# Sparse attention in a decoder kernel: alternating PSUM pairs for the first scores, a later key spreading, and the second thresholds in one piece

## The reference

```python
def sparsemax(x):
    x = x - jnp.max(x, axis=-1, keepdims=True)
    zs = -jnp.sort(-x, axis=-1)
    L = x.shape[-1]
    rho = jnp.arange(1, L + 1, dtype=x.dtype)
    cssv = jnp.cumsum(zs, axis=-1) - 1.0
    support = zs > cssv / rho
    k = jnp.maximum(jnp.sum(support, axis=-1, keepdims=True), 1)
    tau = jnp.take_along_axis(cssv, k - 1, axis=-1) / k.astype(x.dtype)
    return jnp.clip(x - tau, 0.0)
...
scores = jnp.einsum('bhqd,bhkd->bhqk', qh, kh) * scale
attn = sparsemax(scores)
out = jnp.einsum('bhqk,bhkd->bhqd', attn, vh)
...
return out @ Wo + bo
```

## Time and profile before

| what | value |
|---|---|
| median of 3 runs | 1659.28 us (1658.39 to 1662.68) |
| the profiled execution | 1649.06 us |
| its span, first to last instruction | 1647.3 us |
| mean granted TensorE clock over it | 0.795 of full speed |
| stage L3x within the span | about 1332.7 to 1475.5 us |

### The profile page before, as it was taken

The page is one execution under the profiler, slowest core; times in us unless marked ns, Lnnn a source line. Parts: engine busy times, 40 slices in busy tenths (PEclk is TensorE's granted clock), DMA queues, the critical chain, the costliest instruction groups (busy, mean ns, idle before and its releaser), DMA issues. The chain is left out here.

```text
span 1647.3 us, 35633 instructions
## 1 busy us (share of the span) xinstructions
PE 1186.9 (72%) x14064; PEld 904.8 (55%) x14064; DVE 1056.5 (64%) x2853; ACT 625.0 (38%) x1479; POOL 616.3 (37%) x694
## 2 busy tenths in 40 slices
PE   6982518957999779664687843299948875677778
PEld 5652417846788646553455733188825642564556
DVE  4988611148999748824688498243389937766672
ACT  2641103415777646122454321022124434443433
POOL 3437354432333236443233026533343343233320
PEclk9995559979999889676788555599958766777878
DMA  8900035660000085031000000355310000000000
GB/s 272 151 2 2 15 105 164 190 177 4 3 3 3 2 132 80 10 97 46 1 1 2 27 1 17 110 163 169 124 52 1 2 1 1 1 2 1 1 1 27
DMA packets 72010, 89.13 MB, mean 54 GB/s; under 512 B 5823, under 2 KB 59138, under 8 KB 71200
## 3 DMA queue, kind: packets, MB, share of 16 engines
q1 hardware_dynamic: 65824, 76.89, 18.6%
q0 software_dynamic: 6016, 9.93, 1.7%
HBM read 56.55 MB, written 32.69 MB: 54 GB/s over the span
## 5 line engine op out<-in xcount | busy, mean ns | idle before, releaser
L769 POOL TENSOR_TENSOR arena<-arena,small 128x1024 f32<-128x1024 f32 x80 | 154.7, 1939 | 112.1 <-ACT arena L651 65.8
L380 POOL TENSOR_SCALAR var_eps<-moments 128x1 f32<-128x1 f32 (+1 forms) x136 | 35.7, 262 | 356.5 <-DVE moments L373 356.5
L700 ACT ACTIVATE arena<-arena 128x1024 f32<-128x1024 f32 x80 | 84.7, 1058 | 135.0 <-DVE arena L844 134.9
L566 PE MATMUL ps<-arena,q 64*64 64x512 f32 x640 | 102.6, 714 | 40.4 <-issue 17.2
L576 PEld LDWEIGHTS ps<-small,arena 128*128 128x128 f32 x640 | 82.6, 159 | 63.9 <-issue 34.0
L725 ACT COPY arena<-ps 128x512 f32<-128x512 f32 x160 | 87.1, 588 | 68.2 <-PE ps L576 67.6
L576 PE MATMUL ps<-small,arena 128*128 128x128 f32 x640 | 100.5, 308 | 9.7 <-ACT arena L700 9.7
L1608 PEld LDWEIGHTS ps<-expert_ring,arena 128*128 128x128 f32 (+1 forms) x864 | 104.6, 192 | 2.9
L1608 PE MATMUL ps<-expert_ring,arena 128*128 128x128 f32 (+1 forms) x864 | 104.8, 275 | 0.0
L588 PEld LDWEIGHTS ps<-vx,arena 128*64 128x64 f32 x2560 | 90.8, 151 | 16.5 <-issue 13.2
L588 PE MATMUL ps<-vx,arena 128*64 128x18 f32 x2560 | 99.0, 222 | 0.9 <-issue 0.6
(11 more groups left out here) (363 smaller groups left out, 2946.6 us busy)
## 6 DMA issues: line engine op xcount, KB each, us to landing
expert_ring<-L2f_in SPq DMA_DIRECT2D x23, 704.0 KB, 4.2
expert_ring<-L0f_in SPq DMA_DIRECT2D x23, 578.0 KB, 3.9
slots_L0f<-blank SPq DMA_DIRECT2D x1, 8385.0 KB, 51.2
slots_L2f<-blank SPq DMA_DIRECT2D x1, 8385.0 KB, 49.9
small<-small_in SPq DMA_DIRECT2D x1, 4231.5 KB, 19.2
expert_ring<-L1f_in SPq DMA_DIRECT2D x8, 512.0 KB, 3.8
arena<-slots_L0f SPq DMA_DIRECT2D x23, 129.0 KB, 3.3
arena<-slots_L2f SPq DMA_DIRECT2D x23, 129.0 KB, 3.5
```

The source lines that it names most:

```text
L566: last = pe.matmul(c.ps[part(b), m], c.q[part(m), at:at + S], kx(t)[part(m), b * 512:(b + 1) * 512], start=True, stop=True)
L700: act.activation(buf(k), buf(k), ACT.Exp, scale=exp_scale).then_inc(s.probs_ready, 1)
L769: g.tensor_tensor(kx(t).rearrange("p (b h k) -> p b h k", b=2, k=S), bcast(of_tile, 2, HEADS // 2), bcast(bcast(c.w("head_of_row"), 2, S), ...
```

## The change

Four places of `sparse_attention` are edited.

- The scores of tiles 0 to 7 alternate between PSUM banks 0, 1 and banks 2, 3; later tiles use banks 0 and 1 as before. Up to tile 8, `scores(t)` waits for the copy of tile t-2 instead of tile t-1.
- On POOL, the spreading of tile 9 (and so of all later tiles) waits until the scan of the first half has ended (`s.summed`). Tile 8 is still spread ahead of that wait.
- `find_thresholds(1)` moves from the end of DVE's step 8 to the end of step 7, right behind `sum_largest(1)`. PE's `count_open_rows(1)` moves from the end of step 9 to the end of step 8.
- In DVE's step 9, `normalise(7)` moves behind `settle_thresholds(1)` and `less_threshold(8)`.

No instruction that computes is added or removed.

```diff
-    scores_ps = c.ps[:, 0:2].rearrange("p m n -> p (m n)")
+    score_banks = lambda t: 2 * (t % 2) if t < half_tiles else 0
+    scores_ps = lambda t: c.ps[:, score_banks(t):score_banks(t) + 2].rearrange("p m n -> p (m n)")
...
-            if t > 0:
-                pe.wait_ge(s.scored, t)
+            copied = t - 1 if t <= half_tiles else t
+            if copied > 0:
+                pe.wait_ge(s.scored, copied)
             for m in range(2):
                 for b in range(2):
                     at = t % 8 * P + b * S
-                    last = pe.matmul(c.ps[part(b), m], c.q[part(m), at:at + S],
+                    last = pe.matmul(c.ps[part(b), score_banks(t) + m], c.q[part(m), at:at + S],
                                      kx(t)[part(m), b * 512:(b + 1) * 512], start=True, stop=True)
...
-            if k == half_tiles + 1:
+            if k == half_tiles:
                 count_open_rows(1)
...
-            act.copy(z(t), scores_ps).then_inc(s.scored, 1)
+            act.copy(z(t), scores_ps(t)).then_inc(s.scored, 1)
...
         for t in range(1, half_tiles + 2):
+            if t == half_tiles + 1:
+
+                g.wait_ge(s.summed, 1)
             spread_keys(t)
...
                 if k == half_tiles + 1:
-                    normalise(tile_at(k - lag - 1))
                     settle_thresholds(1)
                     less_threshold(tile_at(k))
+                    normalise(tile_at(k - lag - 1))
                 less_threshold(tile_at(k + 1))
...
             if k == half_tiles - 1:
                 sum_largest(1)
-            if k == half_tiles:
                 find_thresholds(1)
```

## The result

The changed kernel took 1646.06 us in the median (1633.62 to 1649.62) against 1660.98 for the kernel before. The ratio is 0.989, with a 95% interval of 0.985 to 0.993. Two later comparisons, on a chip each and with more executions, gave 0.991 (0.9874 to 0.9945) and 0.991 (0.9877 to 0.9948), so some 15 us. Executions that took over 1.5% more than the fastest of the same kernel are left out of all ratios and medians.

What follows compares the result with a forecast made beforehand. No engine bounds the stage everywhere: scores wait for ACT's copy, POOL's spreading blocks DVE, later thresholds alternate between PE and DVE. Gains 5.2 + 3.3 + 2.2 = 10.7 us take 1659.28 to 1648.6; range 1643.5 to 1653.8.

Steps and rivals of the forecast that it cites:

- First edit: First scores: two PSUM pairs take ACT's copy out of the chain, MAX8 blocks follow at 2.04 us; gain 5.2 us.
- the ring: First scores: PE and POOL pass two key buffers back and forth, 1.6 or 2.1 us a tile by the clock.
- Second edit: First thresholds: spreading 9 waits for the scan, so copy, subtraction and scan lose 4.54 us less 0.5 and 0.7; gain 3.3.
- my full-clock case: First thresholds: with PE at full clock, spreading 8 ends at 1363.2, ahead of DVE's copy at 1364.4; nothing lost.
- My ends of 0.6 and 4.5: First thresholds: lowest and highest gain in us from making spreading 9 wait, with all collisions or with none.
- Third edit: Second thresholds in one go: second scan's end to less_threshold(8) takes 11.57 us instead of 13.92; gain taken as 2.2.
- Rival 3: PE's clock improves: spreading 8's collision goes (0.5 us), one more rise of some 4 us saves 3; 1645, chance 0.10.
- Rival 4: PE's clock worsens: the dense stretch from 1396 to 1419 at 1.2 GHz costs 16 us more; 1664.6, chance 0.04.
- Rivals 1, 2 and 5: POOL collisions persist, 1651.3 (0.14); second-threshold change gives nothing, 1650.8 (0.11); tiles' scores still wait, 1653.8 (0.06).

Runs made afterwards that it cites:

- the six passes: Only the last layer's sparse and causal attention, run six times in a row; 1606.3 us with the old sparse attention, 1516.9 and 1521.7 with the changed one.

## Why the prediction was right or wrong

- **First edit, 5.2 us.** Right. Measured 5.25 in the whole kernel, and the MAX8 blocks follow at 2.02, where I had 2.04. PE waits for POOL's keys, which is the ring that I had next in line, and DVE is behind both. That the bound holds at the lower clock is shown for two tiles.
- **Second edit, 3.3 us.** The mechanism was right and the size was off; this is the first step that failed. Measured 4.27. I took off 0.5 for spreading 8 meeting the copy, since the clock could be at 0.50 there as before; it was at 1.00, spreading 8 ended 1.1 us ahead of the copy (1.2 in my full-clock case), and it never met it in the kernels that have both edits (0.27 or 0.28 in every copy). I took off 0.7 for the comparison; it was held up 0.26 (0.64 against 0.38). So 0.26 of the 1.2 taken off was there. My ends of 0.6 and 4.5 held it. The order was as I let it be: the candidates went first at 1.22 us, the maximum passed beside POOL at 1.22, and the comparison waited.
- **The Trainium skill's rule** (SBUF — State Buffer, Who interferes with whom), that two-input DVE instructions and GpSimd's reads shut each other out and reductions never take part, agrees with the trace in the candidates (1.22, with spreading 9 at 2.95 instead of 1.91 beside them), the comparison (0.64) and the maximum (1.22). The copy has one input and was also held up (1.63, 0.87); the page counts copies among the instructions that can take both ports.
- **Third edit, 2.2 us.** Right: 2.2 at the step in the first pair of profiles and 2.4 over the passes. The parts of the sum stand in the timeline: 3.13 for the thresholds, 0.34 until PE starts, then PE's block and projection until add(5) at 1440.65, and 4.12 from the cast to less_threshold(8).
- **Sum, 10.7 us.** The steps gave 11.5 to 11.7. The second step that failed is the one from the part to the program: I let the end of the program gain what the part's chain gains, with an exception only for a later clock that takes some of it back. The runs show 2.6 to 3.4 us a pass more than the steps. On average over the passes they lie in the causal attention (2.9), which I had taken as untouched and in which the granted clock falls otherwise; what lies ahead of tile 1's MAX8, the stretch between the first and the second thresholds, and the tail came out 0.3 us shorter, 0.3 shorter and 0.8 longer, which nearly cancels.
- **The range.** Its lower end allows 1.5 us for the runs' own spread, and single executions scatter by about 6. The interval of the first comparison, put on 1659.28, reaches from 1633.9 to 1647.8. Steps and the 3 us behind them make 14 to 15 of its 18 us; the other 3 to 4 lie within that interval, and the two later comparisons, at 15 us, don't have them.
- **Rival 3, a better clock,** came nearest. Its first half came true: the clock stayed at 1.00 in the first scores, and the collision of spreading 8 went. Its 3 us for a later rise (1645) has the size that was measured; that is luck in part, since I worked it out for a rise of some 4 us and not for the causal attention.
- **Rival 4, slower by the clock,** does not hold for the change, but its mechanism is real: the first edit alone lost 2.6 of its 7.2 us a pass beyond its steps, and single tails cost 5 to 15 us. Rivals 1, 2 and 5 fell with the steps.
- **The base.** I took the profiled execution for the base of the sum. Since the difference was taken off the median, this cost nothing, but the two profiled spans alone would have shown a gain of 1.2 us.

The variant with add(4) ahead of the thresholds is better than both kernels in the six passes, 1502.9 against 1516.9, with 2.3 us a pass as worked out for it; in the whole kernel it can't be told from the changed one (1645.11 against 1643.67 medians, intervals that overlap almost fully).

## What to carry to other kernels

A chain that hands one buffer back and forth is cut by a second buffer, and the new pace is the slowest engine's own time: that can be worked out from one timeline to a few tenths. An engine off the critical path can still hold up the one on it through a shared resource, and its work is cheapest put beside instructions that don't use that resource. Where TensorE's clock moves in the kernel, give the forecast a term of some microseconds for it, either way and for the code behind the change too, and compare repeated passes of the part: single spans of the whole kernel can differ by 20 us in code that is the same.

## What the runs showed of the hardware that was not expected

- The comparison took 0.64 us beside spreading 9 and ended at 1389.22; that spreading's record (2.95 of the 4.86 us shown) ended at 1389.06. If the comparison's own 0.38 us came last, it began 0.2 us before that record ended, so the shared resource seems to come free before the end of POOL's record. This is inferred from the durations.
- The same 397 matmuls cost 15.8 us more of PE in a stretch that stayed at 1.2 GHz for all of its 52.1 us, though PE was busy for 46.02 of them. The other two stretches hold the same matmuls and were granted 0.78 on average, so the higher clock for part of them.
- The causal attention, with the same code, took 111.2 to 120.0 us, and its length went with the number of times the granted clock rose within it. Two passes with a tail of 36.94 us were followed by 119.6 us, and two with 36.98 and 36.99 by 113.5.
- The code ahead of the part, the same in all kernels, took 1332.6 to 1353.2 us. Its mean granted clock was 0.787 to 0.799 and does not put these in order; no run here shows why they differ.
